# Attention scores of two heads on two row tiles of TensorE

## What is computed

```python
h = _layernorm(x, axis=-1) * (1 + ca) + sa
# attention on h: q has 16 heads, k and v have 4, d = 16
scores = jnp.einsum('bhgnd,bhsd->bhns', qg, k) * (1.0 / jnp.sqrt(jnp.float32(d)))
mask = jnp.tril(jnp.ones((T, T), dtype=bool))
att = jax.nn.softmax(jnp.where(mask, scores, -jnp.inf), axis=-1)
y = jnp.einsum('bhns,bhsd->bhnd', att, v)
...
x = x + ga * (y @ Wo + bo)
h = _layernorm(x, axis=-1) * (1 + cb) + sb
# feed-forward on h: rmsnorm, v/wo product, rmsnorm, silu(gate) * up, down; kept only where routed
x = x + gb * _L0_ffn_ref(h, ...)
```

## Time and profile before

| | |
|---|---|
| median of 3 runs | 466.26 us (465.66 to 468.48) |
| span of the profiled execution | 466.8 us |
| PE busy | 437.2 us, 94% |
| PE weight loads | 371.8 us, 80% |
| DVE busy | 353.9 us, 76% |
| ACT busy | 308.4 us, 66% |
| POOL busy | 182.2 us, 39% |

### The profile page before, as it was taken

One profiled execution on the slowest core, in us unless ns is written; L12 is line 12 of the kernel. 1 busy time (PEld: TensorE's weight loads), 2 busy tenths in 40 slices (PEclk: granted clock), 3 DMA queues, 4 the chain that ended last, 5 costly groups with the idle time before them and its releaser, 6 DMA issues. The chain is left out here.

```text
span 466.8 us, 9486 instructions
## 1 busy us (share of the span) xinstructions
PE 437.2 (94%) x3320; PEld 371.8 (80%) x3320; DVE 353.9 (76%) x796; ACT 308.4 (66%) x640; POOL 182.2 (39%) x262
## 2 busy tenths in 40 slices
PE   5887979888989999999999999999999999999996
PEld 5674545686587688997858999999898798999995
DVE  4579968788989488898855889888885766578565
ACT  2298578775588887527697764676768698645441
POOL 6376527410246220214827404523243333325622
PEclk9999899999999999999999999999999999999998
DMA  7921030000000100020021000000010000000001
GB/s 192 333 93 51 3 97 1 2 1 3 0 3 11 43 2 0 2 70 1 27 86 24 2 1 24 1 26 5 20 51 9 24 22 2 25 1 24 22 25 46
DMA packets 16576, 16.04 MB, mean 34 GB/s; under 512 B 4233, under 2 KB 14926, under 8 KB 16530
## 3 DMA queue, kind: packets, MB, share of 16 engines
q1 hardware_dynamic: 16530, 15.44, 10.8%
HBM read 11.09 MB, written 4.21 MB: 33 GB/s over the span
## 5 line engine op out<-in xcount | busy, mean ns | idle before, releaser
L792 PE MATMUL banks<-gTh,guhi 128*128 128x256 f32 x352 | 101.2, 287 | 0.0
L794 PE MATMUL banks<-gTh,gulo 128*128 128x256 f32 x352 | 98.8, 281 | 0.0
L793 PE MATMUL banks<-gTl,guhi 128*128 128x256 f32 x352 | 98.7, 280 | 0.0
L937 ACT ACTIVATE PT<-banks 128x1024 f32<-128x1024 f32 (+3 forms) x96 | 74.5, 810 | 29.8 <-PE banks L708 24.4
L792 PEld LDWEIGHTS banks<-gTh,guhi 128*128 128x128 f32 x352 | 66.4, 189 | 1.6 <-issue 0.7
L1165 DVE TENSOR_REDUCE mxp<-banks 128x2 f32<-128x1024 f32 (+3 forms) x56 | 61.9, 1141 | 6.4 <-PE banks L684 3.9
L793 PEld LDWEIGHTS banks<-gTl,guhi 128*128 128x128 f32 x352 | 66.5, 189 | 0.3
L794 PEld LDWEIGHTS banks<-gTh,gulo 128*128 128x128 f32 x352 | 66.4, 189 | 0.0
L684 PE MATMUL banks<-QKT 128*128 128x512 f32 (+3 forms) x192 | 49.9, 368 | 6.8 <-ACT QKT L915 3.4
L708 PE MATMUL banks<-QKT 128*128 128x512 f32 (+3 forms) x192 | 50.9, 369 | 0.9 <-ACT PT L937 0.4
L708 PEld LDWEIGHTS banks<-QKT 128*128 128x128 f32 x192 | 30.3, 190 | 23.3 <-issue 21.2
(11 more groups left out here) (178 smaller groups left out, 1093.4 us busy)
## 6 DMA issues: line engine op xcount, KB each, us to landing
xres<-in_L_attn_x SPq DMA_DIRECT2D x8, 512.0 KB, 4.4
out_x<-xres SPq DMA_DIRECT2D x16, 256.0 KB, 2.1
wm_st<-in_L_wmod SPq DMA_DIRECT2D x1, 1024.0 KB, 7.9
modB<-mod_scratch SPq DMA_DIRECT2D x4, 256.0 KB, 3.4
wg_st<-in_L_ffn_w_gate SPq DMA_DIRECT2D x1, 704.0 KB, 5.0
wu_st<-in_L_ffn_w_up SPq DMA_DIRECT2D x1, 704.0 KB, 6.2
xres<-in_L_ffn_w_down SPq DMA_DIRECT2D x1, 640.0 KB, 5.7
wm_st<-in_L_wmod SPq DMA_DIRECT2D x1, 512.0 KB, 6.2
```

What stands on the lines that cost most here:

```text
L792: pe.matmul(out_, guhi[:, k, blk, :], gh, start=(m == 0 and k == 0), stop=False)
L793: pe.matmul(out_, guhi[:, k, blk, :], gl, start=False, stop=False)
L794: i = pe.matmul(out_, gulo[:, k, blk, :], gh, start=False, stop=(m == len(blocks) - 1 and k == KB - 1))
L937: act.activation(PT[:, u % 2, 2 * q:2 * q + 2, 0:CH - q0], both("prob", b, n)[:, :, 0:CH - q0], ACT.Exp, scale=float(D) ** -0.5).then_inc( ...
```

## The change

Both passes now address 64 partitions of `QKT` in each matmul, rows 0 to 63 for the even head and 64 to 127 for the odd one, for the weights as for the streamed operand. The zero halves are not read any more, but are still written at the start. The outputs, their banks, the mask matmuls, all waits and the table `ORDER` stay.

```diff
@@ -681,8 +681,9 @@
                     diag = k0 + kn == (qt + 1) * P
                     for m, q in enumerate(at):
                         for e in range(2):
-                            i = pe.matmul(o[:, e, m * kn:(m + 1) * kn], QKT[:, q, qt * P:(qt + 1) * P],
-                                          QKT[:, 2 + 2 * q + e, k0:k0 + kn], start=(m == 0),
+                            rows = slice(e * HR, (e + 1) * HR)
+                            i = pe.matmul(o[:, e, m * kn:(m + 1) * kn], QKT[rows, q, qt * P:(qt + 1) * P],
+                                          QKT[rows, 2 + 2 * q + e, k0:k0 + kn], start=(m == 0),
                                           stop=not diag and m == len(at) - 1)
                     if diag:
                         for e in range(2):
@@ -705,8 +706,9 @@
                     free(kind, n)
                     o = both(kind, b, n)
                     for e in range(2):
-                        i = pe.matmul(o[:, e, 0:CH - q0], QKT[:, 2 + 2 * q + e, j * P:(j + 1) * P],
-                                      QKT[:, q, c * CH + q0:(c + 1) * CH], start=True, stop=True)
+                        rows = slice(e * HR, (e + 1) * HR)
+                        i = pe.matmul(o[:, e, 0:CH - q0], QKT[rows, 2 + 2 * q + e, j * P:(j + 1) * P],
+                                      QKT[rows, q, c * CH + q0:(c + 1) * CH], start=True, stop=True)
                     i.then_inc(S["prob"], 1)
```

## The result

| | median | runs | ratio to the kernel before (95% interval) |
|---|---|---|---|
| before | 466.12 us | 465.66 to 468.48 | |
| changed | 472.56 us | 471.07 to 476.93 | 1.0145 (1.0106 to 1.0183) |
| changed, measured again in 11 runs | 469.88 us | 468.18 to 473.58 | 1.0078 (1.0051 to 1.0105) |

The change makes the kernel slower, by 3.5 us in the larger measurement and 6.4 in the first. The forecast was 465.5 us. The changed kernel scatters over 5 us, and it scatters with the granted clock: of the 11 runs the fastest (468.18) has a mean clock of 0.985, the slowest two (473.54, 473.58) 0.967, while the kernel before beside them has 0.990 to 0.998.

A forecast was written before the change was run, and what follows sets the result against it. PE was taken to bound the kernel, DVE setting the pace in stretches of the first two batches. Saving 34.9 us, adding 35.0 and gaining 1 turned the profile's 466.8 into 465.9; 0.5 less for the median gave 465.5, range 448 to 482.

The forecast's parts named there:

- what a switch is made of: On PE, changing between whole and half rows costs an emptying plus an uncovered load, 0.20 us, less beside masks.
- The slot saved: In score matmuls, each couple takes one matmul's slot instead of two, 0.23 us for 512 columns; 34.9 us in all.
- the emptying of 0.09: At each change of array shape on PE, the array empties before the next matmul starts, losing 0.09 us.
- the uncovered load of 0.10: After a change of shape on PE, the first weights load with nothing to cover them, taken as 0.11 us.
- weight loads of two tiles overlap: At entry to half rows, a couple's two weight loads run together, so a switch costs 0.20 us, not up to 0.31.
- the distance from a lone couple of 512 to the next start: On PE's timeline, the next whole-array matmul was to start 0.32 us behind a couple of 512.
- the first and second: Couples' loads or streams overlap only in part, 476 or 481 us, chance 0.17; no overlap at all, 500 us, chance 0.08.
- the third: Entering or leaving half rows needs no emptying, only loads are uncovered: 446.5 us, or 440 if loads hide; chance 0.14.
- the sums cancel: Over all score matmuls, 34.9 us of saved slots against 35.0 us of added switches.
- the prediction's prices: For each group of couples: slots saved, less 0.20 us per edge, 0.13 entering after a mask, 0.10 leaving to one.
- What is left: Difference between stretches: long groups between `pv` steps of the first batches win, later lone couples lose; 1 us gained.
- The last sentence of the prediction: Signs of being wrong: couples starting apart, edges at 0.12 us, or granted clock below its full level after 60 us.

The follow-up runs named there:

- e7: Kernel before, plus one extra 128-column matmul over only 64 rows at the start of each of the 48 gate steps: 480.46 us, ratio 1.0277.
- e8: Kernel before, plus one extra 128-column matmul over all 128 rows at the start of each of the 48 gate steps: 470.07 us, ratio 1.0073.
- e2: Changed kernel with half rows only in batch 0, all 128 rows in batches 1 to 3: 468.83 us, ratio 1.0053.
- e1: Changed kernel with half rows only in batches 1 to 3, all 128 rows in batch 0: 467.36 us, ratio 1.0023.
- e6: Changed kernel with half rows only in batches 1 to 3, and there only in groups that gain by the predicted prices: 462.61 us, ratio 0.9925.
- e9: Changed kernel with half rows only in batches 1 to 3, and there only in groups that lose by the predicted prices: 470.72 us, ratio 1.0089.
- e10: Changed kernel with half rows only in groups that gain by the predicted prices, in all batches including batch 0: 465.89 us, ratio 0.9992.
- e4: Changed kernel plus two extra whole-array matmuls at the start of each of batch 0's 20 `max` steps: 473.98 us, ratio 1.0157.
- e11: Kernel before plus two extra whole-array matmuls at the start of each of batch 0's 20 `max` steps: 468.43 us, ratio 1.0065.

## Why the prediction was wrong

**Right: what a switch is made of.** The slot saved, the emptying of 0.09, the uncovered load of 0.10, and that weight loads of two tiles overlap, all came out. Only the distance from a lone couple of 512 to the next start was not 0.32 but 0.42, since its recorded start does not wait for the uncovered load. None of the three rivals happened: couples overlap (against the first and second), and the emptying is there at row tiles (against the third), 0.09 us at the entry. The page "TensorEngine Tiling (Array Packing)" of the Trainium skill, Key Properties, says that a change of tiling mode drains TensorE; for row tiles the trace now agrees, with that 0.09 us. Worked out from the starts in both traces, for the 78 groups after 90 us that stand without a gap, the two edges of a group cost on average 0.37 us between two products (I had 0.40), 0.27 from a product to a mask (0.30), 0.33 from a mask to a product (0.33), 0.33 from a transpose to a product (0.40). e7 and e8 confirm the size end to end.

**Right in the whole, wrong in the parts: that the sums cancel.** By batches the prediction's prices do not cancel: they give 3.4 us gained in batch 0 and 9.5 - 6.0 = 3.5 lost in batches 1 to 3. Measured were 2.4 lost (e2) and 0.9 lost (e1). In batches 1 to 3 the signs held but the sizes were too large: e6 has 3.8 of 6.0, e9 4.7 of 9.5. In part the prices are a little high; the 78 gapless groups lost 3.5 us where my prices give about 5.3. For the rest the waits may absorb both sides: followed by the same DVE instructions in both traces, e9 is only 0.1 us behind at 139 us, where the prices give some 1.3, and 4.3 at the end; in the last stretch, after 355 us, where PE has next to no gap, it loses 1.1 us of a priced 1.4. No experiment took that last reason apart, so it is argued, not shown.

**Wrong: the step "What is left", 1 us gained, and with it the granted clock, which no term held.** The prediction took the first batches as places where a cheaper PE stream costs nothing and long groups gain. In batch 0 the opposite happened: the stream became shorter, the granted clock was at 1.2 GHz for 15 to 20 of 26 us (0.71 in e2's profile is 2 x 0.29 x 26 = 15 us at half, 0.61 is 20), and 2.4 us were lost (e2), 3.3 where only winning groups were changed (e10 against e6). That DVE paces those stretches was right, and at a full clock half rows cost nothing there: e1's profile, with batch 1 in half rows, is level with before through batch 1's `max` stretch (0.0 to 0.4 us ahead from 99 to 132 us of the trace of before, clock 1.00), and e2's is level in batch 0 until the clock falls. What remains open is the 1.2 us at a full clock that e4 has over e11.

I had seen the warning and had not priced it: the fifth slice of the clock row of before reads 8, and the stretch from 34 to 60 us has 0.93, so the clock was already not full there. The last sentence of the prediction names a falling clock as a sign of being wrong, but only after 60 us, while most of the fall came before, and with no chance and no price. It deserved the place of a rival that ends slower. The 472.56 us of the first measurement lies inside the range, 448 to 482, but the ranges for slower rested on rivals that did not happen, so that is luck.

## What to carry to other kernels

Matmuls on part of the array gain only in long unbroken groups: price each edge of a group (here 0.2 us, or 0.1 where the next load is uncovered or small anyway) against the slots that it saves, and keep the whole array where the group loses. Here that choice alone, over all batches, gained nothing (e10, ratio 0.9992); with batch 0 left out as well it turned 3.5 us lost into 3.8 us gained (e6). So before a PE stream is shortened where another engine sets the pace, look at the granted clock of that stretch: where it is already below full, less PE work can make everything on PE there slower.

## What the runs showed of the hardware

- Two fp32r matmuls on 64 rows each and in different PSUM banks stream together: two couples of 512 between two `pv` steps take 0.46 us less than before. Their weight loads overlap too, with recorded starts 4 ns apart in the median: 0.42 to 0.43 us from the start of a lone couple of 512 to the next whole-array matmul includes one uncovered load, one stream and the emptying.
- A change from whole to half rows costs the same emptying as one to strips of 32 columns, 0.09 us. Half rows and strips exchange places at no more than what leaving strips cost before: from the last `pv` matmul of 512 columns to the couple behind it 0.52 us in both traces.
- In these profiles the clock fell with what PE is given to stream: the same couples issued twice held it at 0.87 from 34 to 60 us, issued once at 0.61 and 0.69.
